# Eight down products for nine in each routed slot of a mixture of experts, with the down weights in units of a lead scale

## The reference, cut to what matters

```python
def dequant_fp4(packed, scales, gs=128):
    codes = packed[..., :, None, :] >> shifts[:, None] & 15
    w = FP4_LUT[codes].reshape(new_shape)
    return w * jnp.repeat(scales, gs, axis=-2)
...
act = swiglu(jnp.einsum('th,ehi->eti', x, w_gu))      # 512 -> 2 x 384
w_d = dequant_fp4(down_packed, down_scales)           # 384 -> 512
y_e = jnp.einsum('eti,eih->eth', act, w_d)
out = jnp.einsum('te,eth->th', combine, y_e)
```

## Time and profile before

| | |
|---|---|
| median of 3 runs | 690.94 us (689.84 to 693.83) |
| profiled execution, its own time | 687.41 us |
| its span, first to last instruction | 685.6 us |
| busy: TensorE, VectorE, ScalarE, GpSimd | 92%, 71%, 47%, 48% |
| mean granted TensorE clock | 0.982 of full |
| the chain that ended last: TensorE's share | 80%, of it 45% of the span at line 1207, 22% at line 1235 |
| moved by DMA | 93.7 MB |

### The profile page before, as it was taken

One profiled execution on the slowest core, in us unless ns is written; L12 is line 12 of the kernel. 1 busy time (PEld: TensorE's weight loads), 2 busy tenths in 40 slices (PEclk: granted clock), 3 DMA queues, 4 the chain that ended last, 5 costly groups with the idle time before them and its releaser, 6 DMA issues.

```text
span 685.6 us, 17258 instructions
## 1 busy us (share of the span) xinstructions
PE 629.7 (92%) x4394; PEld 382.1 (56%) x4395; DVE 488.1 (71%) x1271; ACT 325.3 (47%) x558; POOL 326.2 (48%) x506
## 2 busy tenths in 40 slices
PE   3768969999998999999999999999999999999992
PEld 2444536557554656565665656566565656656561
DVE  6979779895766858588888767778588878767110
ACT  1763567331343455454544554454554545455541
POOL 3621834100334465564646555464655656565432
PEclk9999989999999999999999999999999999999997
DMA  8780101128157875768587594847767587654533
GB/s 234 202 247 2 63 31 64 62 54 276 49 172 160 189 173 127 176 123 195 110 203 176 126 223 74 226 85 201 168 135 183 117 199 158 152 86 77 93 39 39
DMA packets 49841, 93.72 MB, mean 137 GB/s; under 512 B 8840, under 2 KB 16776, under 8 KB 49816
## 3 DMA queue, kind: packets, MB, share of 16 engines
q0 software_dynamic: 16128, 38.35, 30.3%
q1 hardware_dynamic: 32936, 55.04, 27.5%
q10 hardware_dynamic: 752, 0.04, 0.1%
HBM read 65.16 MB, written 28.24 MB: 136 GB/s over the span
## 4 chain that ended last, share of the span: by engine, by line
PE 80%; DVE 6%; DMA 3%; ACT 3%; POOL 3%; issue 2%; SPq 1%; DVEq 0%; POOLq 0%; ACTq 0%
PE gu_ps L1207 45%; PE bank L1235 22%; PE bank L1247 4%; PE bank L1221 4%; DMA dn_sc<-dn_scale_halves 2%; PE bank L1262 1%; DMA room_a<-in_ctx 1%; PE gu_ps L1167 1%; POOL room_a L462 1%; PE bank L1164 1%; PE bank L1191 1%; DVE stats L725 1%; POOL X L445 1%; DVE X L1000 1%; ACT mix_room L581 1%
## 5 line engine op out<-in xcount | busy, mean ns | idle before, releaser
L1207 PE MATMUL gu_ps<-wgu,mix_room 128*128 x1728 | 305.9, 327 | 2.7 <-DVE tick L950 1.6
L1207 PEld LDWEIGHTS gu_ps<-wgu,mix_room 128*128 128x128 f16 x1728 | 166.5, 98 | 114.7 <-issue 7.5
L1235 PE MATMUL bank<-wdn,aT 128*128 (+1 forms) x792 | 186.2, 380 | 3.2 <-ACT aT L629 2.6
L530 POOL DMA_INDIRECT out<-mix_room,idx_s x72 | 122.9, 1707 | 32.4 <-issue 30.9
L629 ACT ACTIVATE aT<-bank 128x768 f16<-128x768 f16 x88 | 71.2, 809 | 139.5 <-PE bank L1221 136.2
L1235 PEld LDWEIGHTS bank<-wdn,aT 128*128 128x128 f16 x792 | 77.6, 98 | 88.8 <-issue 3.6
L501 POOL TENSOR_TENSOR pool_tick<-ones 128x1 f32<-128x1 f32 x144 | 35.7, 248 | 163.6 <-DMA out<-mix_room,idx_s 84.0
L991 DVE SCALAR_TENSOR_TENSOR act<-gu_ps,wslot,sg x72 | 44.5, 618 | 96.4 <-ACT sg L615 84.8
L622 ACT ACTIVATE acth<-act 128x384 f16<-128x384 f32 x88 | 46.0, 523 | 120.1 <-DVE act L991 120.1
L512 POOL DMA_INDIRECT room_b<-token_rows,idx_g x72 | 76.0, 1055 | 12.3 <-issue 3.6
L927 DVE TENSOR_TENSOR wgu<-dq_code,gu_sc 128x768 f16<-128x768 f16 x136 | 72.5, 574 | 2.3
(11 more groups left out here) (157 smaller groups left out, 588.1 us busy)
## 6 DMA issues: line engine op xcount, KB each, us to landing
dn_sc<-dn_scale_halves SPq DMA_DIRECT2D x34, 384.0 KB
dn_raw<-in_L_ffn_down_packed SPq DMA_DIRECT2D x48, 256.0 KB
gu_sc<-gu_scale_halves SPq DMA_DIRECT2D x34, 192.0 KB
X<-in_x SPq DMA_DIRECT2D x4, 1024.0 KB, 8.4
token_rows<-room_a SPq DMA_DIRECT2D x16, 256.0 KB, 2.2
out<-X SPq DMA_DIRECT2D x4, 1024.0 KB, 11.1
gu_raw<-in_L_ffn_gate_up_packed SPq DMA_DIRECT2D x16, 192.0 KB
gu_raw<-in_L_ffn_gate_up_packed SPq DMA_DIRECT2D x16, 191.9 KB
```

What stands on the lines that cost most here:

```text
L530: nc.gpsimd.indirect_dma_start(out[:, :], bass.IndirectOffsetOnAxis(idx_s[:, b:b + 1], 0), y_sb[:, b, :], None, compute_op=ALU.add).then_i ...
L1207: mm = nc.tensor.matmul(ps[b][:, 0:I], x(xp * HC + c), wgu[:, w, wp, c, col:col + I], start=(c == 0 and xp == 0 and wp == 0), stop=(c == H ...
L1235: mm = nc.tensor.matmul(y_ps[0 if shared else b][:, :], aT[:, b, ap, t, :], wdn[:, w, wp, t, :], start=(n == 0), stop=(n == 3 * IC - 1))
```

## The change

For each expert and column the scale of the first chunk (the lead scale; where it is far smaller than the others, a value built from them) is taken out of all three: the down scales become ratios, that of the first chunk a number with no low half. So the product high x low of the first chunk goes, and `down` has eight products in a routed slot. The shared expert keeps nine. VectorE makes no low halves for the first 512 columns (the whole first part, a third of the second). y comes out of PSUM without the lead scale; GpSimd multiplies it by the lead scales of its expert, a 128x512 float32 tile that SP loads behind the expert's other loads, into room that the transposed tokens have left.

Around that: the copies of row numbers for gathers and scatters go to ScalarE (two in each slot, one at the slot's start, one in `take_y`); the gather waits for ScalarE's copy; one register load per scatter brings both the expert and the count of line 526, packed by two more steps in the slot tables. The routed down scales are no longer split at the start but loaded apart, made into exponents and scales (`lead_exponents`, `lead_scales`, 15 steps of 64 columns) beside the shared expert's last dequantization, into ratios (`down_ratios`, 6 steps of 192 columns) behind shared slot 4, and stored and loaded back by SP ahead of the eleventh row store. 22 of 64 one-column memsets at VectorE's start go.

```diff
+        def load_lead(sp, n, landed):
+            at_e = bass.ds(n - 1, 1)
+            sp.dma_start(lead_y[:, at_e, :], lead_dram[at_e].unsqueeze(0).broadcast_to([P, 1, H])).then_inc(landed, 16)
...
+        def load_dn_scales(sp, buf, n, landed):
             for hl in range(2):
-                sp.dma_start(dn_sc[:, buf, hl, :, :],
-                             dn_s_dram[hl, n].unsqueeze(0).broadcast_to([P, IC, H])).then_inc(ld_w[buf], 16)
+                t0 = 0 if hl == 0 or (isinstance(n, int) and n == 0) else 1
+                sp.dma_start(dn_sc[:, buf, hl, t0:, :],
+                             dn_s_dram[hl, n, t0:].unsqueeze(0).broadcast_to([P, IC - t0, H])).then_inc(landed, 16)
+
+        def load_scales(sp, buf, n):
+
+            load_gu_scales(sp, buf, n)
+            load_dn_scales(sp, buf, n, ld_w[buf])
...
-        LEAD = 64
+        LEAD = 42
...
-            load_scales(sp, 1, 1)
+            for t in range(IC):
+                sp.dma_start(dn_all[:, t, :], dn_scales[:, t, :].rearrange("e (b n) -> e b n", n=HB)).then_inc(ld_dn, 16)
+            sp.wait_ge(st_sc, 32)
+            load_gu_scales(sp, 1, 1)
             for i in range(NT):
 
+                if i == 10:
+                    sp.wait_ge(dn_split, 1)
+                    for hl in range(2):
+                        for t in range(hl, IC):
+                            sp.dma_start(dn_s_dram[hl, 1:, t, :].rearrange("e (b n) -> e b n", n=HB),
+                                         dn_h[:, hl, t, :]).then_inc(st_dn, 16)
+                    sp.dma_start(lead_dram.rearrange("e (b n) -> (e b) n", n=HB), lead_s[:, :]).then_inc(st_dn, 16)
+                    sp.wait_ge(st_dn, 16 * (2 * IC - 1 + 1))
+                    load_dn_scales(sp, 1, 1, ld_lead)
+                    for n in (1, 2):
+                        load_lead(sp, n, ld_lead)
                 sp.wait_ge(xh_ready, i + 1)
                 sp.wait_ge(xl_ready, i + 1)
                 sp.dma_start(rows_dram[i * P:(i + 1) * P, 0:H],
...
             load_expert(sp, gu_packed[2], dn_packed[2], 1, 3)
+            load_lead(sp, 3, ld_w[1])
...
-            def hold_wait():
-
-                nc.gpsimd.tensor_tensor(pool_tick[:, :], ones[:, 0:1], ones[:, 0:1], ALU.mult)
+            def hold_wait(k):
+
+                nc.gpsimd.tensor_tensor(pool_tick[:, k:k + 1], ones[:, 0:1], ones[:, 0:1], ALU.mult)
 
             def gather(s, b):
 
                     pool.wait_ge(tx_done, s - 1)
                     pool.wait_ge(wslot_done, s - 1)
                 pool.wait_ge(route_ready, 1)
-                nc.gpsimd.tensor_copy(idx_g[:, b:b + 1], tok[:, bass.ds(s, 1)]).then_inc(idx_g_ready, 1)
-                pool.wait_ge(idx_g_ready, s + 1)
-                hold_wait()
+                if isinstance(s, int) and s < 2:
+                    nc.gpsimd.tensor_copy(idx_g[:, b:b + 1], tok[:, bass.ds(s, 1)]).then_inc(idx_g_ready, 1)
+                    pool.wait_ge(idx_g_ready, s + 1)
+                else:
+                    pool.wait_ge(idx_g_ahead, s - 1)
+                hold_wait(s if isinstance(s, int) else b)
                 nc.gpsimd.indirect_dma_start(xg[:, b, :], None, rows_dram[:, :],
                                              bass.IndirectOffsetOnAxis(idx_g[:, b:b + 1], 0)).then_inc(xg_ld[b], 16)
 
             def add(s, b):
 
                 pool.wait_ge(st_out, 16 * (B + 1))
-                if not isinstance(s, int) or s >= 2:
-                    pool.wait_ge(added[b], 8 * (s - b))
-                nc.gpsimd.tensor_copy(idx_s[:, b:b + 1], tok[:, bass.ds(s, 1)]).then_inc(idx_s_ready, 1)
+                both = pool.value_load(others_i[0:1, bass.ds(s, 1)], min_val=16 * E, max_val=8 * SLOTS * E + E - 1)
+                others, e = both // E, both % E
+                pool.wait_ge(yev_done, s + 1)
+                nc.gpsimd.tensor_tensor(y_sb[:, b, :], y_sb[:, b, :],
+                                        lead_y[:, bass.ds(e, 1), :].rearrange("p k n -> p (k n)"), ALU.mult).then_inc(y_scaled, 1)
+                if not isinstance(s, int):
+                    pool.wait_ge(added[1 - b], others)
+                elif s >= 1:
+                    pool.wait_ge(added[1 - b], 8 * (s + b))
                 pool.wait_ge(idx_s_ready, s + 1)
-                if isinstance(s, int):
-                    if s >= 1:
-                        pool.wait_ge(added[1 - b], 8 * (s + b))
-                else:
-                    others = pool.value_load(others_i[0:1, bass.ds(s, 1)], min_val=16, max_val=8 * SLOTS)
-                    pool.wait_ge(added[1 - b], others)
-                pool.wait_ge(yev_done, s + 1)
-                hold_wait()
+                pool.wait_ge(y_scaled, s + 1)
+                hold_wait(6 + b)
                 nc.gpsimd.indirect_dma_start(out[:, :], bass.IndirectOffsetOnAxis(idx_s[:, b:b + 1], 0), y_sb[:, b, :],
                                              None, compute_op=ALU.add).then_inc(added[b], 16)
             for s in range(4):
                 gather(s, s % 2)
             pool.wait_ge(route_ready, 2)
+            pool.wait_ge(ld_lead, 64)
...
             def take_y(r, b):
-                a.wait_ge(y_done, NT + r + 1)
                 if not isinstance(r, int) or r >= 2:
                     a.wait_ge(added[b], 8 * (r - b))
-                nc.scalar.activation(y_sb[:, b, :], y_ps[b][:, :], ACT.Copy, scale=1.0 / W_SCALE).then_inc(yev_done, 1)
+                nc.scalar.activation(idx_s[:, b:b + 1], tok[:, bass.ds(r, 1)], ACT.Copy).then_inc(idx_s_ready, 1)
+                a.wait_ge(y_done, NT + r + 1)
...
-            def slot(r, b, rows=True):
+            def slot(r, b, rows=True, list_ahead=True):
+                if list_ahead:
+                    nc.scalar.activation(idx_g[:, b:b + 1], tok[:, bass.ds(r + 2, 1)], ACT.Copy).then_inc(idx_g_ahead, 1)
                 copy_aT(r + (NT - 1), 1 - b)
...
-            slot(2 * inner + 2, 0)
-            slot(2 * inner + 3, 1, rows=False)
+            slot(2 * inner + 2, 0, list_ahead=False)
+            slot(2 * inner + 3, 1, rows=False, list_ahead=False)
...
-            v.wait_ge(ld_sc, 64)
+            v.wait_ge(ld_sc, 48)
...
+            def lead_exponents():
+
+                EXPONENT, TINY, DEEP = 0x7F800000, 2.0 ** -100, 2.0 ** -20
+                v.wait_ge(ld_dn, 16 * IC)
+                step(nc.vector.tensor_scalar(e_rest.bitcast(I32), s1.bitcast(I32), EXPONENT, None, ALU.bitwise_and), wait=False)
+                step(nc.vector.tensor_scalar(up.bitcast(I32), s2.bitcast(I32), EXPONENT, None, ALU.bitwise_and), wait=False)
+                step(nc.vector.tensor_scalar(e_lead.bitcast(I32), s0.bitcast(I32), EXPONENT, None, ALU.bitwise_and))
+                step(nc.vector.scalar_tensor_tensor(e_rest, e_rest, TINY, up, ALU.max, ALU.max))
+                step(nc.vector.scalar_tensor_tensor(keep, e_rest, DEEP, e_lead, ALU.mult, ALU.is_le), wait=False)
+                step(nc.vector.scalar_tensor_tensor(reach, e_rest, DEEP, e_lead, ALU.mult, ALU.max))
+
+            def lead_scales():
+
+                step(nc.vector.reciprocal(up, reach), wait=False)
+                step(nc.vector.tensor_scalar(other, keep, -1.0, 1.0, ALU.mult, ALU.add))
+                step(nc.vector.tensor_tensor(up, up, e_rest, ALU.mult), wait=False)
+                step(nc.vector.tensor_tensor(other, other, e_rest, ALU.mult))
+                step(nc.vector.scalar_tensor_tensor(own, up, 1.0, s0, ALU.max, ALU.mult))
+                step(nc.vector.tensor_tensor(own, own, keep, ALU.mult))
+                step(nc.vector.tensor_tensor(own, own, other, ALU.add))
+                step(nc.vector.reciprocal(inv, own), wait=False)
+                step(nc.vector.tensor_scalar(lead_s[:, :], own, 1.0 / W_SCALE, None, ALU.mult))
+
+            def down_ratios():
+
+                step(nc.vector.tensor_tensor(dn_all, dn_all, inv.unsqueeze(1).broadcast_to([P, IC, HB]), ALU.mult))
+                step(nc.vector.tensor_scalar(dn_top, dn_all, SPLITTER, None, ALU.mult))
+                step(nc.vector.tensor_tensor(dn_rest, dn_top, dn_all, ALU.subtract))
+                step(nc.vector.tensor_tensor(dn_top, dn_top, dn_rest, ALU.subtract))
+                step(nc.vector.tensor_scalar(dn_h[:, 0], dn_top, W_SCALE, None, ALU.mult))
+                nc.vector.scalar_tensor_tensor(dn_h[:, 1], dn_all, W_SCALE, dn_h[:, 0], ALU.mult,
+                                               ALU.subtract).then_inc(dn_split, 1)
...
+                    step(nc.vector.tensor_scalar(slot_f[:, :], slot_f[:, :], float(E - 1), None, ALU.min), wait=False)
                     step(nc.vector.tensor_tensor(first_of_expert[:, :], first_of_expert[:, :], before_s[:, :], ALU.mult))
-                    step(nc.vector.tensor_scalar(others_i[:, :], first_of_expert[:, :], 16.0, None, ALU.max))
+                    step(nc.vector.tensor_scalar(first_of_expert[:, :], first_of_expert[:, :], 16.0, None, ALU.max))
```

(59 more changed lines are left out.)

26 lines of the change are left out of this document (16 added, 10 removed).

## The result

728.88 us, the median of 4 runs (725.95 to 732.0), against 690.39 of the kernel before on the same chip (4 runs, 686.94 to 693.83): the ratio is 1.0569, with a 95% interval of 1.0531 to 1.0607. The change is 38.5 us slower. The sign was forecast, the size was not: 702, in a range that ended at 716.

What follows compares the result with a forecast made beforehand. TensorE was taken as the bound, VectorE close behind; -15.6 + 22.8 + 1.65 + 0.45 + 1.3 + 1.0 = +11.6 us on 687.4 gave 699, or 702 on the median, range 694 to 716.

Steps and rivals of the forecast that it cites:

- The products: TensorE, routed slots: one down product of nine goes in each of 72 slots, 0.216 us each, 15.6 us gained.
- the experts that end on VectorE: Four-slot experts whose next gate-up already waits for VectorE in the kernel before; five such places lose 2.3 us.
- The rest: Loads 1.65, slot tables 0.45, tail 1.3 and SP's wait for the ratios 1.0 us, all added time.
- the tail's 1.3: End of the kernel: the last scatter waits for the last multiply, 1.3 us added.
- What the multiply costs VectorE: Dequantizing slots: GpSimd's multiply meets VectorE's stream every time, 0.75 us a meeting, 22.8 us lost in all.
- The count of demands: VectorE's time per slot against TensorE's 6.40 us: 6.45, 6.40, 7.48 and 8.45 us in an expert's four slots.
- Rival 4: VectorE's dequantization: a meeting costs the whole multiply, 1.2 us, giving 724 us; chance 0.04.
- The gather behind ScalarE's copy: GpSimd's order in a slot: the gather needs ScalarE's copy of its row numbers, so GpSimd gathers first and multiplies second.

Runs made afterwards that it cites:

- d: The kernel before with eight products in a routed slot (high x low of the first chunk left out) and nothing else; 681.05 us, ratio 0.988.
- c: The change with GpSimd copying the gather's row numbers itself again and its multiply cut from 512 columns to one; 687.64 us, ratio 0.9974.
- f: The change with GpSimd copying the gather's row numbers itself again and its multiply cut to 256 of 512 columns; 697.91 us, ratio 1.0157.
- a: The change with GpSimd copying the gather's row numbers itself again, the multiply whole; 721.46 us, ratio 1.0483.
- g: The kernel before with the gathers' row numbers copied by ScalarE behind the copy of y; nine products, no multiply; 706.33 us, ratio 1.0273.
- h4: The change with VectorE scaling y out of PSUM, early gathers, one wait less per scaling step, no parity arithmetic or leading memsets; 762.26 us, ratio 1.1077.

## Why the prediction was wrong

**The products** were right: 1.73 us for eight, and with the experts that end on VectorE d was to gain 15.6 - 8.9 + 2.3 = 9.0 us; it gained 8.9.

**The rest** (loads, slot tables, SP, tail), taken as 4.4, is 6.6 by c less d, near enough with d's runs between 678.8 and 683.8; most of the tail's 1.3 is not in it, since c's last scatter waits for a multiply of one column. The first routed activation starts 4.5 us later in after (194.11 for 189.59), but at 189.73 in c, which has the same work ahead of it. The granted clock from 40 to 100 us was 0.79 in this execution of after and 0.91 in those of before and c, so the delay is not shown to be the change's.

**The step that failed first is "What the multiply costs VectorE".** The text said that the two meet in every dequantizing slot, which holds, and that a meeting costs 0.75 us, "0.91 less 0.15 for the two copies". It costs 1.22. The count of demands was sound for meetings: with one of 0.47 it gives 9.7 us over c, and f showed 10.3; with 1.03 it gives 30.0, and a showed 33.8. With 1.22 in place of 0.75 the prediction's own sum would have come to +34.7, 726 us, outside its range. The size put into it was read from one place, where VectorE's step came up 0.23 us behind the start of a subtraction of 1.32. What was left of that was 1.09, and the loss was 0.91; so even that row stood near the full price, and there was no reason to take 0.15 off. Rival 4, the whole multiply at 1.2 us, gave 724 and had a chance of 0.04. The Trainium skill, "SBUF — State Buffer", section "Who interferes with whom", says that the engine that issued second is fully blocked. The trace agrees on the length, 1.22 us beside 1.28. On who yields it decides nothing: L1019 is shown to begin 0.32 us ahead of the multiply and stood all the same, but its undisturbed 0.36 would have ended only 0.04 behind the multiply's start, and starts on GpSimd are rough in a profile.

**The second step was not in the sum at all.** The gather behind ScalarE's copy was used to order GpSimd's work and never priced on TensorE. The lead could be read from the kernel before, whose issue comes 2.35 us behind the transposes and 10.9 ahead of the need; moving it behind the copy of y took 4 us of that, where the pieces of after's chain for it last 7.0 to 8.3 us. Alone it costs 18.4 us (g); beside the multiply 7.4, perhaps because both make the same slots late. How much of the 7.4 is waiting for rows (11.2 us of waits in after), and how much the longer meeting (1.22 for 1.03, some 9 us by the count), was not separated; each alone would be more than the whole, so they can't simply be added.

The measured terms: -8.9 for the products, +6.6 for the rest, +33.8 for the multiply and +7.4 for the gather give +38.9, against +38.5.

## What to carry to other kernels

An elementwise step moved to GpSimd beside a VectorE without gaps was paid here in VectorE's time, up to nearly its whole length (1.22 of 1.28 us in the change, 1.03 of 1.36 in a, 0.47 of 0.83 in f); room on GpSimd didn't help. When the wait ahead of a DMA's issue changes, compare issue to need with issue to landing, even where the new wait is only for a short copy. And when a loop's code grows or moves, look at the instruction queue's packets before blaming the new work.

## What the runs showed of the hardware that was not expected

Where VectorE's loop lies in its code decides whether code is fetched again at each turn: 26 or 27 packets more, and five stands of 5.8 to 8.4 us, or of 12.1 to 13.0 with a start at 661. All ten kernels without a stand start their loop at one and the same instruction, and end it anywhere from 1007 to 1037; the four that start elsewhere all stood, h4 too, which ends at 1013 as before does. How far the start may move was not mapped. The Trainium skill, "Runtime: NRT & Kernel Launch", section "Instruction fetch mechanics", has a taken branch wait for a fetch where its target lies outside the two pages held; the trace agrees in that packets come at every turn where VectorE stands and at none where it doesn't, and puts a price on it. The 22 leading memsets that the change drops are part of that: without them its loop starts at the same instruction as before's.

A multiply of half the columns took 0.83 us on GpSimd and not half of 1.36.
